# Sum passes of a graph network: the bf16 split of gathered rows through PSUM, shared by ScalarE and VectorE

## The reference, cut to what matters

```python
def _L2_gnn_ref(x, edge_index):
    src, dst = (edge_index[0], edge_index[1])
    msgs = jnp.take(x, src, axis=0)
    return jax.ops.segment_sum(msgs, dst, num_segments=x.shape[0])

def _L3_gnn_ref(x, edge_index, edge_attr, u, batch, W1, b1, W2, b2):
    row, col = (edge_index[0], edge_index[1])
    msg = jnp.concatenate([x[row], edge_attr], axis=1)
    msg = msg @ W1 + b1
    agg = jax.ops.segment_sum(msg, col, num_segments=x.shape[0])
    out = jnp.concatenate([x, agg], axis=1)
    return out @ W2 + b2
...
    h = jnp.maximum(_layernorm(x, axis=-1), 0.0)
    x = x + _L2_gnn_ref(h, edge_index)
    h = jnp.maximum(_layernorm(x, axis=-1), 0.0)
    x = x + _L3_gnn_ref(h, edge_index, edge_attr_32, L3_gnn_u, batch0, L3_gnn_W1, L3_gnn_b1, L3_gnn_W2, L3_gnn_b2)
```

## Time and profile before

| | |
|---|---|
| Runs shown | 10403.08, 10408.71, 10415.81 us; median 10408.71 |
| Profiled execution | 10406.76 us, of which the span of the trace is 10405.1 us |
| Busy over the span | PE 7742.2, VectorE 6690.1, ScalarE 5664.1, GpSimd 7146.6 us |
| First to last gather of the sum pass | 8748.2 to 9363.5 us |
| First to last gather of the last pass | 9673.6 to 10351.2 us |

### The profile page before, as it was taken

The page is one execution under the profiler, slowest core; times in us unless marked ns, Lnnn a source line. Parts: engine busy times, 40 slices in busy tenths (PEclk is TensorE's granted clock), DMA queues, the critical chain, the costliest instruction groups (busy, mean ns, idle before and its releaser), DMA issues. The chain is left out here.

```text
span 10405.1 us, 367947 instructions
## 1 busy us (share of the span) xinstructions
PE 7742.2 (74%) x123397; PEld 6624.2 (64%) x123398; DVE 6690.1 (64%) x15383; ACT 5664.1 (54%) x15112; POOL 7146.6 (69%) x9555
## 2 busy tenths in 40 slices
PE   6666666646578999889998899967777755446666
PEld 5444444434467888778887788867666645445566
DVE  7444444456536999638885388853599974654686
ACT  2555555546536999629995399942588841002000
POOL 2777777777746888548885588830388856774786
PEclk9555555555589999899998999979999988558767
DMA  6222222259998888697775977769988858667887
GB/s 248 67 68 70 66 66 70 67 174 329 320 283 300 274 276 274 173 361 243 240 239 168 348 240 239 238 130 405 337 257 255 256 192 308 198 184 283 279 257 197
DMA packets 1408416, 2335.53 MB, mean 224 GB/s; under 512 B 311979, under 2 KB 826300, under 8 KB 1381310
## 3 DMA queue, kind: packets, MB, share of 16 engines
q1 hardware_dynamic: 1078046, 1293.68, 40.2%
q0 software_dynamic: 217824, 515.78, 16.9%
q10 hardware_dynamic: 112320, 523.03, 12.5%
HBM read 1381.15 MB, written 905.59 MB: 220 GB/s over the span
## 5 line engine op out<-in xcount | busy, mean ns | idle before, releaser
L639 POOL DMA_INDIRECT by_src<-sort_rec,slots x1560 | 1540.1, 987 | 651.3 <-issue 651.3
L1328 POOL DMA_INDIRECT NEAR<-spread_f,gather_ids_l x1368 | 1371.4, 1002 | 253.6 <-issue 179.3
L1453 ACT ACTIVATE z_l<-z_l,sizes_l 128x64 f32<-128x64 f32 x5472 | 1376.6, 342 | 0.2 <-DVE sizes_l L1417 0.2
L773 PE MATMUL bank<-hots_t 104*128 104x512 bf16 (+3 forms) x1568 | 613.4, 467 | 720.0 <-ACT junk L598 719.9
L773 PEld LDWEIGHTS bank<-hots_t 104*128 104x128 bf16 x1568 | 218.5, 139 | 1018.7 <-ACT junk L598 831.9
L1536 PE MATMUL bank<-wm_diag,zr_t_l 128*128 128x128 f32 x5472 | 796.3, 289 | 2.9 <-issue 2.9
L1536 PEld LDWEIGHTS bank<-wm_diag,zr_t_l 128*128 128x128 f32 x5472 | 665.4, 192 | 158.7 <-issue 158.7
L1490 PE MATMUL bank<-m_l,hot_wide_l 128*128 128x64 f32 x5472 | 743.2, 279 | 0.0
L1183 POOL COPY unit_near_a<-NEARB 128x192 bf16 x1368 | 415.0, 347 | 426.2 <-PE bank_bf L1168 220.3
L1515 PE MATMUL bank<-NEARB,hot_t_l 128*128 x16416 | 641.4, 194 | 48.5 <-ACT hot_t_l L1443 15.3
L1490 PEld LDWEIGHTS bank<-m_l,hot_wide_l 128*128 128x128 f32 x5472 | 666.7, 192 | 0.0
(11 more groups left out here) (386 smaller groups left out, 26799.9 us busy)
## 6 DMA issues: line engine op xcount, KB each, us to landing
spread_f<-unit_rows_a ACTq DMA_DIRECT2D x342, 512.0 KB, 5.9
hot_t_l<-dst_hots_t SPq DMA_DIRECT2D x456, 256.0 KB
hot_wide_l<-dst_wide SPq DMA_DIRECT2D x456, 256.0 KB
unit_hot_a<-src_hots_t SPq DMA_DIRECT2D x342, 256.0 KB, 4.1
dst_hots<-NEAR SPq DMA_DIRECT2D x228, 256.0 KB
dst_hots_t<-hot_t_l SPq DMA_DIRECT2D x228, 256.0 KB
dst_wide<-hot_wide_l SPq DMA_DIRECT2D x228, 256.0 KB
NEAR<-dst_hots SPq DMA_DIRECT2D x456, 128.0 KB
```

Source lines behind the costliest of these rows:

```text
L639: pool.indirect_dma_start(out=by_src, out_offset=bass.IndirectOffsetOnAxis(ap=slots[h][:, j:j + 1], axis=0), in_=rec[h][:, j, :], in_offse ...
L773: pe.matmul(to, lhsT=cols[:, t * P:width], rhs=cols[:, 0:width], start=True, stop=False, skip_group_check=True)
L1328: pool.indirect_dma_start(out=far_in[h % WA][:, g * GT:(g + 1) * GT, :].rearrange("p j f -> p (j f)"), out_offset=None, in_=spread_f, in_o ...
L1453: last = act.activation(z[h % WA][:, t, :], z[h % WA][:, t, :], ACT.Relu, scale=sizes[h % WA][:, 2, 0, t:t + 1])
```

## The change

ScalarE gets two jobs. It copies the gathered rows in two halves of 512 columns to PSUM (`whole`, in `banks[4]` and `banks[5]`), and it makes the middle part (`middle`, bf16 in SBUF) by copying `rest` with a conversion to bf16. VectorE subtracts in halves as well: `rest[k] = whole[k] - top(rows_in)` from PSUM and SBUF into PSUM (`banks[6]` and `bank_bf`), and `last_of = rest[k] - middle` from PSUM and SBUF into SBUF. The second pair of subtractions stands behind the window sums in VectorE's order. TensorE waits for both parts and reads `middle` in place of the upper halves of `rest`. The split of the edge features (L2392, L2397), the gathers, the loads and the window sums stay as they were. Both calls of `sum_pass` change.

```diff
@@ def sum_pass(name, with_edges):
-            s = {n: sem(f"{name}_{n}") for n in ("ids", "acc_ps", "rest", "last", "rest_e", "last_e")}
+            s = {n: sem(f"{name}_{n}") for n in ("ids", "acc_ps", "whole", "rest", "second", "last", "rest_e", "last_e")}
...
-                rest = [state[:, (WU + k) * RT:(WU + k + 1) * RT].rearrange("p (t f) -> p t f", f=D) for k in range(2)]
+                HT = UG * GT // 2
+                whole = [x_.rearrange("p (t f) -> p t f", f=D) for x_ in (banks[4][:], banks[5][:])]
+                rest = [x_.rearrange("p (t f) -> p t f", f=D) for x_ in (banks[6][:], bank_bf[:].bitcast(F32))]
+                middle = [state[:, WU * RT + k * RT // 2:WU * RT + (k + 1) * RT // 2].bitcast(BF16)
+                          .rearrange("p (t f) -> p t f", f=D) for k in range(2)]
@@ VectorE, a tick
                         if p := part(0):
                             h, st, n, nth = p
                             arrived(dve, rows_ready, h, nth, UG)
-                            at_least(dve, s["acc_ps"], n - 2)
-                            dve.tensor_tensor(rest[h % 2][:], rows_in[h], top(rows_in[h]), ALU.subtract).then_inc(s["rest"], 1)
-                            dve.wait_ge(s["rest"], n)
-                            dve.tensor_tensor(last_of[h % 2][:], rest[h % 2][:], top(rest[h % 2]),
-                                              ALU.subtract).then_inc(s["last"], 1)
+                            for k in range(2):
+                                dve.wait_ge(s["whole"], 2 * (n - 1) + k + 1)
+                                at_least(dve, s["last"], 2 * (n - 2) + k + 1)
+                                dve.tensor_tensor(rest[k], whole[k], top(rows_in[h])[:, k * HT:(k + 1) * HT, :],
+                                                  ALU.subtract).then_inc(s["rest"], 1)
                         if p := part(2):
...
+                        if p := part(0):
+                            h, st, n, nth = p
+                            at_least(dve, s["acc_ps"], n - 2)
+                            for k in range(2):
+                                dve.wait_ge(s["second"], 2 * (n - 1) + k + 1)
+                                dve.tensor_tensor(last_of[h % 2][:, k * HT:(k + 1) * HT, :], rest[k],
+                                                  middle[h % 2][:, k * HT:(k + 1) * HT, :], ALU.subtract).then_inc(s["last"], 1)
@@ ScalarE, new
+                @block.scalar
+                def _(act):
+                    def tick(part):
+                        if p := part(0):
+                            h, st, n, nth = p
+                            arrived(act, rows_ready, h, nth, UG)
+                            for k in range(2):
+                                at_least(act, s["rest"], 2 * (n - 2) + k + 1)
+                                act.activation(whole[k], rows_in[h][:, k * HT:(k + 1) * HT, :],
+                                               ACT.Copy).then_inc(s["whole"], 1)
+                            at_least(act, s["acc_ps"], n - 2)
+                            for k in range(2):
+                                act.wait_ge(s["rest"], 2 * (n - 1) + k + 1)
+                                act.activation(middle[h % 2][:, k * HT:(k + 1) * HT, :], rest[k],
+                                               ACT.Copy).then_inc(s["second"], 1)
+
+                    rolling(act, steps, WU, 0, tick)
@@ TensorE, a tick
-                            pe.wait_ge(s["last"], n)
-                            rows = (top(rows_in[h]), top(rest[h % 2]), last_of[h % 2][:])
+                            pe.wait_ge(s["second"], 2 * n)
+                            pe.wait_ge(s["last"], 2 * n)
+                            rows = (top(rows_in[h]), middle[h % 2][:], last_of[h % 2][:])
```

## The result

The changed kernel takes 10308.91 us (median of 4 runs, 10303.77 to 10316.05) against 10412.26 us for the kernel before (4 runs). The ratio is 0.9903 with a 95% interval of 0.9891 to 0.9914: 1.0% faster, where 0.7% (10335 us) was forecast. The profiled execution took 10303.77 us with a span of 10302.0.

The account below looks back on a forecast made before the run. GpSimd's queue was taken to pace both passes. Terms: -33.5 (sum pass), -50 (last pass), +3 (VectorE), +4.4 (latency), +3 (DMA), together -73 us: 10335 us, own range 10310 to 10358, wide range 10293 to 10380.

Parts of the forecast that it names:

- The bound, and the cause of the long gathers: Both passes: GpSimd's queue sets the pace; gathers wait for VectorE instructions with two SBUF operands, 34.2 us in the sum pass.
- The new form holds nothing: New subtractions, one operand in PSUM: hardly hold gathers (11 to 22 ns before); sum pass mean under 0.97 us.
- VectorE's load: Last pass: a VectorE tick of 5.22 us fits under GpSimd's 5.41; 3 us taken for waits of 0.08 each.
- ScalarE, latency, tails: Both passes: ScalarE's copies mostly hidden, rows to last part 4.5 us, +2.2 us per pass end; 4 and 6 us given up.
- Nothing queues: Slots of both passes: gathers, landing, split and products take some 17 us, where four steps give 21.6.
- a sign of being wrong: GpSimd's idle time after the change: waits for TensorE there would show the prediction wrong; 3.4 us before.
- The last pass: the term that was mis-sized: Last pass gathers and index copies: 44.3 and 12 us go, 6 given up in the tail, term -50 us.
- The sum pass came as forecast: Sum pass gathers and index copies: up to 37.7 us go, about 4 given up at the end, term -33.5 us.
- the edge split's 37.6: Last pass: 37.6 us of gather excess under the unchanged edge instructions L2392 and L2397, taken to stay.
- a shift of phase: Last pass, best bound: the edge split's stalls go as well, -90 us in place of -50.
- rival 2: Last pass: edge split's stalls go too, or the copies gain in full; total 10293 us; chance 0.10.
- Rival 1: Last pass: VectorE becomes the bound; at a 5.74 us tick 23 us gained, not 50; whole about 10360; chance 0.18.

Follow-up runs that it names:

- the second half-edge run: Changed kernel with the edge split on 16 of the 32 edge features, repeated on a slow chip; ratio 1.002 (0.9999 to 1.0042) to the kernel before.

## Why the prediction was right, and where a term was not

*The bound, and the cause of the long gathers.* This was right. The sum pass lost 34.4 us of gather time and 3.5 of index copies, where 34.1 and 3.6 were computed, and the runs with operands back in SBUF bring the stall back under whichever pair has both there. The gate pass already had such a case, which the prediction did not tell apart: its longest gather, 1202 ns, is not under L2115 but under L2106, a subtraction with both operands in SBUF. Matched again, 42 gathers under L2106 have a mean excess of 124 ns, and 166 under L2115 (the prediction has 124 of them) 21 ns.

*The new form holds nothing.* This was right: 989 ns is the longest gather of the sum pass. The remark of the Trainium skill ("SBUF — State Buffer", Who interferes with whom) that a subtraction was not seen to stall descriptor generation does not hold for these gathers (1.28 us under a subtraction, 0.95 beside it); its rule on two SBUF inputs against a GpSimd instruction that reads SBUF does.

*VectorE's load.* 5.22 us was worked out from the earlier trace rows, 5.20 is measured. The 0.08 us that each of the four was allowed for a wait on the other engine is shown by no row that the prediction names, and the 3 us taken for it did not come: the new instructions take 0.69 us and stand 0.60 apart. By these rows the 62 cycles that the Trainium skill ("VectorE: DVE Perf Modes", The TRN2 errata) adds for a PSUM source are not paid here.

*ScalarE, latency, tails.* The last step of the sum pass takes 3.8 us from its first subtraction (9336.73) to the end of the second pair, with ScalarE's first copy 4.5, as forecast. Of the 34.0 and 71.5 us that the gathers gained, the ends of the passes and the longer chain together took back 3.6 in the sum pass and 9.0 in the last, where 4 + 2.2 and 6 + 2.2 had been put down. "Nothing queues" was wrong for the last pass: once VectorE sets its pace, the slots fill, and GpSimd waits 13.7 us for TensorE. The prediction named such waits as a sign of being wrong, and the sign was right about one thing: the step is no longer GpSimd's.

*The last pass: the term that was mis-sized.* The sum pass came as forecast, 30.4 us up to its last product against 33.5 - 2.2; some 10 us of the 103 between the two profiled executions lie outside both passes, and the rest of the difference is here, 62.5 us against about 42. The forecast kept "the edge split's 37.6" us as a cost on top of GpSimd's queue, put its step at 5.41 us, and treated VectorE at 5.22 as a bound that could only take gain away. The gathers lost 62.6 us instead of 44.3, and the step is 5.25. The stalls under L2396 and L2401 came down to 19 us (451.9 - 456 x 0.949), without a change in those instructions. The experiments show what they follow: with VectorE's tick as the pace (steps of 5.25, 5.42 and 5.15 us for three ticks) the stalls take up most of the distance to GpSimd's own 5.03 and no more. In the stretch above, the gathers that start under L2396 meet it near its end. That the two queues fall into step in this way is read from the traces and was not tried by itself. In the kernel before they did not: VectorE's tick was 5.21 us there too, and the step stood at 5.88 to 5.94. There the row split held gathers as well, GpSimd came out later than VectorE, and a stall was a delay of the pace itself; what decides between the two cases is not shown. I had the mechanism in my best bound, as "a shift of phase", and gave it 0.10 with rival 2; half of what that bound allowed came (18.4 of 37.6 us). Rival 1 named the right engine as the new bound, but at a tick of 5.74 and with a loss. At the 5.22 that I had worked out myself, a pass at VectorE's pace is shorter than the one I forecast (5.41 a step), not longer.

## What to carry to other kernels

When GpSimd issues gathers back to back, compare the mean with the median of their duration, and match the long ones with what VectorE runs 0.14 us after they start; a subtraction with both operands in SBUF is then paid twice, and routing one operand through PSUM with an idle ScalarE takes one of the payments away. A stall between two engines that both run in a steady cycle should not be carried over as a sum of microseconds without a second look: work out each engine's cycle without it as well. In the changed form the longer of the two (5.20 us) was the step to within 0.05 us. That is no rule for every case. In the kernel before it would have given 5.21 us where 5.9 was measured; there, instructions with two SBUF operands took 3.8 us of VectorE's tick, against 1.4 us now. A gain in one queue is worth what the next queue leaves, and the next queue may be another on another chip.

## What the runs showed of the hardware that was not expected

The stall of a gather is sharp: the wait ends with the VectorE instruction, counted from 0.14 us after the gather's start, to within 0.02 us in the rows shown. Adding 0.20 us of VectorE work that holds no gather raised the gathers' stalls from 21 to 39 us.

Chips differ by 11.6% on this program (10423 against 11637 us for the same kernel), and the order of the two versions differs with them. TensorE stops between its own products in the two passes on the slow ones, but most of the difference lies ahead of them: the sum pass starts at 9699 us in the second half-edge run, and at 8757 in the changed kernel on the fast chip.
